# Second layer of a transformer kernel: the products with the values of four heads in two batches (four and six score units) in place of three (four, four and two)

## The reference

```python
h = _layernorm(x)                                   # per sequence: 512 x 256
qkv = einsum('bsd,ed->bse', h, W_qkv)               # 16 heads of 16 columns
q, k = _rope(q), _rope(k)
scores = einsum('bhqd,bhkd->bhqk', q, k) / sqrt(16)  # 512 x 512 per head, causal
attn = softmax(scores, axis=-1)
out = einsum('bhqk,bhkd->bhqd', attn, v)
x = x + einsum('bsd,ed->bse', out, W_o)
```

## Time and profile before

| what | value |
|---|---|
| time, median of 3 runs (range) | 3097.34 us (3094.24 to 3098.24) |
| the profiled execution: time, span | 3094.82 us, 3093.1 us |
| busy share of the span: PE, PE weight loads, DVE, ACT, POOL | 93%, 66%, 64%, 48%, 31% |
| eight second-layer stretches | 517 us together |

### The profile page before, as it was taken

The page is one execution under the profiler, slowest core; times in us unless marked ns, Lnnn a source line. Parts: engine busy times, 40 slices in busy tenths (PEclk is TensorE's granted clock), DMA queues, the critical chain, the costliest instruction groups (busy, mean ns, idle before and its releaser), DMA issues. The chain is left out here.

```text
span 3093.1 us, 53525 instructions
## 1 busy us (share of the span) xinstructions
PE 2884.6 (93%) x18384; PEld 2056.4 (66%) x18384; DVE 1980.4 (64%) x6275; ACT 1483.6 (48%) x3132; POOL 958.1 (31%) x1700
## 2 busy tenths in 40 slices
PE   6999899989999899999999989998999989999877
PEld 5666676667766677666776667666676666766654
DVE  5666557675586656766666766677566676665644
ACT  2554344464445644455445554445544554445433
POOL 1233232432333313333233332233223332333231
PEclk8999999999999999999999999999999999999989
DMA  3111001001110010100111001110011000110000
GB/s 121 33 33 31 27 26 37 19 18 33 35 33 19 24 37 26 32 24 19 37 32 33 17 26 37 33 31 14 27 39 32 26 18 23 32 32 18 14 8 29
DMA packets 58700, 91.42 MB, mean 30 GB/s; under 512 B 19904, under 2 KB 32704, under 8 KB 58176
## 3 DMA queue, kind: packets, MB, share of 16 engines
q1 hardware_dynamic: 58432, 88.01, 9.6%
HBM read 81.68 MB, written 5.24 MB: 28 GB/s over the span
## 5 line engine op out<-in xcount | busy, mean ns | idle before, releaser
L1839 ACT ACTIVATE PR<-work 128x512 f32<-128x512 f32 (+1 forms) x1088 | 640.3, 598 | 715.6 <-PE work L1164 608.9
L1438 DVE CUSTOM_DVE_ANT_0 work<-work,KEEPB 128x128 f32<-128x128 f32 (+3 forms) x1536 | 665.8, 477 | 95.6 <-PE work L1128 94.1
L1954 POOL TENSOR_SCALAR_AFFINE_SELECT PR<-PR 128x256 f32<-128x256 f32 (+1 forms) x960 | 362.0, 381 | 872.7 <-ACT PR L1839 868.4
L1128 PE MATMUL work<-BIG 96*128 96x448 f32 (+8 forms) x1664 | 454.6, 364 | 31.8 <-DVE NMX L1438 17.4
L1162 PE MATMUL work<-BIG 99*128 99x512 f32 (+4 forms) x1152 | 420.0, 365 | 11.0 <-DVE BIG L1419 8.6
L1943 POOL TENSOR_TENSOR TOK<-AB 128x256 f32<-128x256 f32 (+1 forms) x320 | 216.6, 677 | 636.7 <-DVE AB L1400 601.6
L1198 PE MATMUL outs<-PR,ONES 128*32 128x512 f32 (+4 forms) x2304 | 407.7, 461 | 0.0
L1419 DVE TENSOR_TENSOR BIG<-work,BIG 96x512 fp32r<-96x512 f32 (+1 forms) x320 | 191.5, 604 | 324.3 <-ACT BIG L1724 324.0
L1128 PEld LDWEIGHTS work<-BIG 96*128 96x128 f32 (+1 forms) x1664 | 278.5, 199 | 157.6 <-issue 64.1
L1163 PE MATMUL work<-BIG 96*128 96x512 f32 (+4 forms) x1152 | 382.7, 332 | 0.0
L1164 PE MATMUL work<-BIG 96*128 96x512 f32 (+4 forms) x1152 | 380.6, 330 | 0.0
(11 more groups left out here) (178 smaller groups left out, 4620.1 us busy)
## 6 DMA issues: line engine op xcount, KB each, us to landing
NRM<-park SPq DMA_DIRECT2D x112, 192.0 KB, 3.1
WKW<-w_kw_dram SPq DMA_DIRECT2D x64, 256.0 KB, 2.7
WSEL<-w_sel_dram SPq DMA_DIRECT2D x64, 256.0 KB, 3.0
R<-park SPq DMA_DIRECT2D x72, 64.0 KB, 2.0
HN<-x_dram SPq DMA_DIRECT2D x8, 512.0 KB, 4.8
X<-x_dram SPq DMA_DIRECT2D x8, 512.0 KB, 3.9
out_dram<-X SPq DMA_DIRECT2D x7, 512.0 KB, 3.2
R<-park SPq DMA_DIRECT2D x16, 192.0 KB, 3.0
```

The costliest lines, as they stand in the source:

```text
L1128: last = mm(ps[:, col:col + n], q, k, start=(i_mm == 0), stop=(i_mm == len(u["mm"]) - 1))
L1438: last = v.tensor_tensor_reduce(ps[:, lo:hi], ps[:, lo:hi], KEEPB[:, T - (hi - lo):T], -1.0, -NEG, ALU.add, ALU.min, dst)
L1839: a.activation(PR[0:rows, j % NP, :], ps[0:rows, :], ACT.Exp).then_inc(exp_ready, 1)
L1954: gp.affine_select(blocks, blocks, [[0, len(cols)], [1, P]], ALU.is_ge, 0.0, base=0, channel_multiplier=-1).then_inc(exp_masked, 1)
```

## The change

`QUAD_PV` says which score units a batch of products takes. The batch of units 4 to 7 and that of units 8 and 9 become one.

```diff
-QUAD_PV = [QUAD[0:4], QUAD[4:8], QUAD[8:10]]
+QUAD_PV = [QUAD[0:4], QUAD[4:10]]
 PRODUCTS = [NPAIR * NPV, NPAIR // 2 * len(QUAD_PV)]
```

## The result

The changed kernel takes 3119.21 us (median of 4 runs, 3116.26 to 3121.38), the kernel before 3096.82 us beside it (4 runs, 3094.24 to 3098.24). The ratio is 1.0073 with an interval of 1.0055 to 1.0090: slower by 17 to 28 us. Forecast were 18.6 us and 3116 us.

What follows compares the result with a forecast made beforehand. In quads 0 to 2 a loop from the last batch through `out` and DMA back to PE sets the pace. 14.6 us for passes 0 to 5 plus 2.0 and 2.0 make 18.6 us, forecast 3116 us, range 3101 to 3125.

Steps and rivals of the forecast that it cites:

- The loop sets the pace: Quads 0 to 2: last batch, `out`, gather, `recip`, spread, `scale`, reductions, PE again; `out` to `recip` 4.43 us, nearly all DMA.
- Exponential 12 waits for the merged batch: On ACT: exponential 12 writes unit 4's slot, so it waits for the merged batch (1.50 us), with `out` behind it.
- Quad 0, 1.35 us: Passes 0 to 5: merged batch starts only with mask 9, `out` 1.35 us late; 8.1 us over six passes.
- Quad 1, 0.28 us left of 0.6: Unit 12 waits for `mt_out`, `out` 0.6 us late; cover by ACT's exponentials leaves 0.28 us a pass.
- quad 2, 1.0 us: PE idles for `mt_out` ahead of unit 12, losing 0.86 us; `out` 1.07 us late; 1.0 us taken between them.
- signs of being wrong: Unchanged DVE waits for the gather, a batch well under 1.4 us, or PE waiting for banks that ACT holds.
- Quad 3 gains 0.2 us a pass: PE is full and no exponential of the pass follows, so the saved drain comes through: -0.2 us a pass.
- Fixed 0.14 us per batch: On PE: each batch has a fixed 0.14 us for entering and leaving the four-column-group form; merging saves one.
- Passes 6 and 7, 2.0 us each: Last two second-layer passes, with other work woven in: 2.0 us slower in each.
- rivals, 1: The DMA loop has play: delays of `out` are absorbed, only PE's loss stays; 5 to 10 us slower; chance 0.16.
- 2 and 3: Rivals: nothing measurable, 3091 to 3103 us, chance 0.08; faster because the drain decides, 3090 us, chance 0.04.
- 4 (a bank held too long by exponential 12): Much slower: exponential 12 holds its PSUM bank, which unit 14 needs, 0.9 to 2.2 us longer; 3127 us; chance 0.07.

Runs made afterwards that it cites:

- out_late: Kernel before, its three batches untouched, with `out` and its gather of quads 0 to 2 issued later, behind exponential 13: 3137.99 us, ratio 1.0141.
- late_slot: late_middle with the exponentials of units 12 to 15 waiting for the last batch instead of the middle one: 3115.87 us, 1.0069 against the kernel before.
- late_middle: Kernel before with three batches, that of units 4 to 7 issued right ahead of the last one, behind unit 12: 3105.29 us, ratio 1.0038.
- m_q0: Kernel before with the merged batch only in quad 0 of each second-layer pass: 3102.30 us, ratio 1.0030.
- late_mask9: late_middle with the middle batch waiting for mask 9, as the merged one does: 3107.46 us, 1.0044 against the kernel before.
- m_q12: Kernel before with the merged batch only in quads 1 and 2: 3110.36 us, ratio 1.0047.
- m_q3: Kernel before with the merged batch only in quad 3: 3093.26 us, ratio 0.9999.
- three_ahead: Kernel before with three batches, the last one, `out` and its gather issued ahead of unit 12 and its exponential: 3088.16 us, ratio 0.9980.
- after_var: Changed kernel with DVE's two variance steps of passes 0 to 5 moved behind quad 0's exponential 13: 3130.48 us, 1.0115 against the kernel before.

## Why the prediction was right

The sign, the mechanism and the size hold: 22.4 us measured (17 to 28) against 18.6 forecast.

1. *The loop sets the pace, and `out` to `recip` can't shrink.* Right: 4.43 us before and after, and `out_late` shows alone that a late `out` is paid nearly in full (4.65 of 4.97 us in pass 0, where the clock is the same). What I had no term for is the clock: where the longer waits brought it down, the loop cost more than the delay.
2. *Exponential 12 waits for the merged batch, and `out` behind it.* Right: 2.34, 1.23 and 1.00 us of wait, 24 times, and `late_slot` against `late_middle` puts 9.6 us on it.
3. *Quad 0, 1.35 us.* 1.24 by the table; `m_q0` alone costs 9.3 us, against 8.1 us for passes 0 to 5 and a part of passes 6 and 7. The batch does start where mask 9 lets it, 18.55 us behind the first exponential of pass 0 before and after (655.16 - 636.61 and 658.21 - 639.66). But the mask was only the last of several waits close together (0.20 us for `mt_out`, 0.56 us for DVE's reductions, 0.24 us for the mask): without it unit 12's wait for DVE's reductions would have let the batch start only some 0.3 us sooner (`late_mask9` against `late_middle`, 0.36 us), which the forecast doesn't mention.
4. *Quad 1, 0.28 us left of 0.6, and quad 2, 1.0 us.* This is the term that was mis-sized: `m_q12` costs 14.5 us, where these two and pass 7 were 6 x 1.28 + 1.85 = 9.5 us. I missed that ahead of unit 12 stands another matmul, the pair's maxima (L1128, at 669.47 above), which needs the bank that `mt_out` reads. So not one but two instructions stand behind the wait, and PE starts the batch at 670.13 instead of some 0.3 us sooner. It is also a wait for a bank that ACT holds, one of the three things that I had named as signs of being wrong, if a small one. Measured for `out` 0 to `out` 1 is +0.83 us. By the steps it was 0.6, which is then given back in part before `out` 2. Taken to `out` 2, the three columns give 1.24 + 0.83 + 0.66 = 2.73 us, against 1.35 + 0.28 + 1.07 = 2.70 forecast: in passes 0 to 5 the errors cancel, which is luck. After `out` 2 the forecast had -0.27 us (0.07 us taken off in quad 2, and quad 3's 0.2); the trace has -0.19. That leaves 6 x 2.54 = 15.2 us, against 14.6 us.
5. *Quad 3 gains 0.2 us a pass.* -0.34 by `m_q3`'s table, -0.19 in the whole; the time of `m_q3` can't tell it from zero.
6. *Fixed 0.14 us per batch.* The size is right, the rule isn't: it is per change of form (`late_middle`). That didn't alter the sum here, since before the batches stood apart; it alters what the change is good for.
7. *Passes 6 and 7, 2.0 us each.* Not confirmed one by one. From first exponential to first exponential of the next pass, the second layer's passes grew by 2.65, 2.52, 3.12, 5.45, 2.77, 0.72, -0.96 and (pass 7, to the end) 4.51 us, 20.8 us in all; the first layer's by 5.7 us, of which 3.8 us lie ahead of any changed step, and so are the difference between two executions (the first exponential of all came 0.7 us earlier, which leaves the 3.05 us above). I can't read terms of 2 us out of such columns. What they do say is that pass 6 shows nothing of its +2.0 us: it is 0.96 us shorter (clock over the pass 0.87 before, 0.90 after), and pass 7 grew by more than twice its term. That the two together come to 3.55 us against 4.0 forecast is luck.

Of the rivals, 1 falls with `out_late`, 2 and 3 with the result, and of 4 (a bank held too long by exponential 12) nothing is seen: the new waits on PE are for `mt_out`, DVE's reductions and masks, not for a bank that an exponential holds.

What stays open is how much of the 22.4 us is clock. That `m_q12` costs 14.5 us, when its table gives 6 x 1.48 = 8.9 us for passes 0 to 5 and pass 7 was counted at 1.85, points to it: in the profiled execution, 15.5 us longer in its span, passes 0 to 5 grew by 12.1 us, from first exponential to first exponential of the next pass, and the median leaves out the dear ones. The dearest is pass 3 (3.9 us), where `out` 1 to `out` 2 took 14.41 us at a clock of 0.79 against 11.65 at 1.00; in the changed kernel the same stretch took 14.65 us at 0.80. Against a large share speaks the mean clock of the timed executions: 0.967 for the changed kernel (4), 0.968 for the kernel before (55, beside the experiments). By an estimate, 0.001 less is half speed for 0.002 of 3100 us more, which costs at most 3 us.

## What to carry to other kernels

Before merging two pieces of work, list for each what it waits for and who waits for it: the merged piece has the latest input of both and releases all at the later end, and what is queued behind the released instruction (here the copy of the sums that starts a 4.4 us DMA loop) pays as well. The fixed cost that merging is meant to save may be had by placing the pieces side by side, with their own waits left as they are: here two neighbouring batches took 1.43 us, as one did. Where a loop through DMA sets the pace, move its first instruction forward (`three_ahead`, -0.20%) and don't put work on the engine that its reply comes back to (`after_var`, +1.15%).

## What the runs showed of the hardware

The changes between forms of TensorE's array are charged by the change: 0.14 us for an excursion into the four-column-group form, with one batch in it or two (1.00 + 0.57 us apart, 1.43 us side by side).

Waits of 1.35 to 2.07 us on PE inside an otherwise full stretch were, in some passes, followed by slower matmuls. The timeline of PE in pass 3 of the changed kernel:

```profile
1813.12 0.50 PE L1128 MATMUL work<-BIG 128*128 128x256 f32 x2 [2.07 <-DVE NMX L1438]
...
1817.39 2.79 PE L1217 MATMUL outs<-PR,NRM 128*32 128x384 f32 x24
```

And the busy times there (columns as in rows 2):

```profile
1812.00:1816.00 4.00, 2.59 (x12) 1.56 (x12) 2.60 (x11) 2.46 (x6) 1.23 (x3) 0.88 0.13 47
1816.00:1821.00 5.00, 4.51 (x29) 2.18 (x29) 0.69 (x1) 2.39 (x6) 1.10 (x2) 0.50 0.05 17
```

PE was busy for 2.59 of 4 us, then the granted clock was 0.50, the 1.2 GHz level, and the merged batch took 2.79 us instead of 1.50. It is the pass that grew by 5.45 us. In quad 0 of pass 7 a wait of 2.07 us for DVE was followed in the same way by a batch of 2.36 us, at a clock of 0.71 over 3049 to 3053. In `out_late` PE waited 1.56 us for DVE (L1439, at 1042.56) between `out` 0 and `out` 1 of pass 1; from 1046 to 1048 the clock was 0.50, and a batch took 1.94 us (at 1045.44) instead of 1.07. In pass 0 PE's waits in that stretch are the same to 0.01 us (1.56 us at 662.86), and the clock stayed at 1.00. So a new wait may cost more than its length, and it doesn't every time: the same stretch took 12.3 us at 1.00 and 13.6 to 13.8 us at 0.87 or 0.88. No run sets the clock apart as a cause; the mean clock of the two profiled executions was 0.965 after and 0.968 before.
